# Random-feature attention, the queries' part: ScalarE copies a step's turned features ahead of the next exponentials, VectorE divides one step later

## Chip, cores and metric

The kernel runs on one core of a Trainium2 chip. The time is the device time of one execution in microseconds (us); a kernel's time is the median over its runs.

## What is computed

The reference runs a graph transformer over 1250 nodes of width 512: a layer norm, then a four-layer graph network and, beside it, a "performer" block, and last a mixture of experts. The change is in the performer's attention. Cut to it (8 heads of width 64, 256 random features):

```
def softmax_kernel(x, pmat):
    xp = jnp.einsum('bhnd,df->bhnf', x, pmat)
    xp = xp - jnp.max(xp, axis=-1, keepdims=True)
    return jnp.exp(xp) / math.sqrt(pmat.shape[-1])
...
q_prime = softmax_kernel(q, Pmat)
k_prime = softmax_kernel(k, Pmat)
kv = jnp.einsum('bhnf,bhne->bhfe', k_prime, v)
k_sum = jnp.sum(k_prime, axis=2) + 1e-06
z = 1.0 / jnp.einsum('bhnf,bhf->bhn', q_prime, k_sum)[..., None]
attn = jnp.einsum('bhnf,bhfe->bhne', q_prime, kv) * z
...
x = x + attn @ Wproj + bproj
```

## The kernel before

The program has three stages, one after another, with a barrier of all engines between them: performer(), gnn() and moe(). Within a stage each engine has its own list of instructions, written out by hand, and the lists are tied together by counting semaphores: `then_inc` at a producer, `wait_ge` at a consumer. No scheduler moves anything; an engine runs its list strictly in order, so what stands ahead of an instruction in its list holds it up.

In performer(), attention_pe(), attention_dve() and attention_act() hold the lists of TensorE, VectorE and ScalarE for the attention. First come 20 steps over the keys, which end in the 256 x 64 sums kv and k_sum of each head, turned and copied to SBUF. Then come the 20 steps over the queries (Q_STEPS), with which the change has to do. A step is two heads (one g) and two tiles of 125 nodes (one u). For step n:

- F(n), features(n), TensorE, helper line L956: the queries by the random matrix, into two PSUM banks, n % 2 choosing which two. It waits for E(n-2), which read those banks.
- M(n), highest(n), VectorE, L1096: the negated maximum of each row of 256.
- E(n), ScalarE, L1150: four exponentials with the maximum as bias, into the SBUF buffer kf, two deep. It waits for M(n) and for T(n-2).
- T(n), turn_features(n), TensorE, L1022: eight transposes of the features into PSUM banks 4 and 5. These two banks are not doubled, so that T(n) waits for C(n-1) as well as for E(n).
- C(n), ScalarE, L1144: two copies of the turned features to qf_cols in SBUF, two deep. It waits for T(n) and for A(n-2).
- A(n), attend(n), TensorE, L1037: the products with kv and with k_sum, into bank 6 or 7. It waits for C(n) and, by `out_made`, for D(n-2).
- D(n), divide(n), VectorE, L1108 and L1110: the reciprocal of the denominators and the multiplication into cols.

TensorE's list has, in round n, F(n), T(n-1), A(n-2). After the last round come the projection of the first node tile (project_pe(0), L1061), T(19), project_pe(1), A(18), A(19), and then pe_end() with further projections; VectorE adds each projection to the residual (project_dve, L1070). The letters F, M, E, T, C, A, D are used in all that follows.

Of the kernel before, what the change touches and what calls it, by code (L numbers as in the profile page):

```python
# [144 lines left out]
def performer(c, xbuf, gnn_x, xn_dram, sum_dram, ln_count, cond_parts, cond_w_parts, w, cols, rows,  # L145
# [62 lines left out]
    qf_mm, qf_max, qf_made, qf_turned, qf_cols_made = c.sems("p_qf_mm", "p_qf_max", "p_qf_made", "p_qf_turned",  # L208
                                                             "p_qf_cols_made")
    out_mm, den_made, out_made = c.sems("p_out_mm", "p_den_made", "p_out_made")  # L210
# [4 lines left out]
    with ExitStack() as ctx:  # L215
# [55 lines left out]
        qf_cols = shared[:, 0:2 * 4 * 2 * P].rearrange("p (u e a n) -> p u e a n", u=2, e=2, a=2)  # L271
# [39 lines left out]
        def split_dve(i):  # L311

            v = c.dve
            which, i = divmod(i, 5)
            rest, parts = ((cond[:, :], c_split), (cond_w, w_split))[which]
            if which == 0 and i == 0:
                v.wait_ge(cond_made, 3)
                v.wait_ge(q_mm, GROUPS)
            if which == 1 and i == 0:
                v.wait_ge(cond_w_in, 128)  # L320
            if i % 2 == 0:
                if i:
                    v.wait_ge(split_step, 2 * which + i // 2)
                v.tensor_copy(parts[i // 2], rest).then_inc(part_made, 1)
            else:
                v.wait_ge(part_made, 3 * which + i // 2 + 1)
                v.tensor_tensor(rest, rest, parts[i // 2], ALU.subtract).then_inc(split_step, 1)
# [613 lines left out]
        def kf_out(n):  # L941

            return psum[0:P, 2 * (n % 3) * BANK:(2 * (n % 3) + 2) * BANK].rearrange("p (e a f) -> p e a f", e=2, a=2)

        def qf_out(n):

            return psum[0:P, 2 * (n % 2) * BANK:(2 * (n % 2) + 2) * BANK].rearrange("p (e a f) -> p e a f", e=2, a=2)

        def qf_turned_out(e):
            return psum[0:128, (4 + e) * BANK:(4 + e) * BANK + 4 * P].rearrange("p (a n) -> p a n", a=2)  # L950

        def kf_slot(n, e, b):
            return 4 * (n % 2) + 2 * e + b
# [111 lines left out]
        def project_dve(t):  # L1065
            v = c.dve
            if t == 0:
                v.wait_ge(bp_added, NT)
            v.wait_ge(o_mm, t + 1)
            v.tensor_tensor(x[:, t, :], x[:, t, :], c.bank(t % 2, D, P), ALU.add).then_inc(o_added, 1)  # L1070
            v.wait_ge(o_added, t + 1)
            h_stats_dve(t)

        def attention_dve():
            v = c.dve
            for n in range(K_STEPS + S_LAG):
                if n < K_STEPS:
                    v.wait_ge(kf_mm, n + 1)
                    if n >= 2:
                        v.wait_ge(kf_made, 4 * (n - 1))  # L1080
                    v.tensor_reduce(mx[:, 4 * (n % 2):4 * (n % 2) + 4].rearrange("p (e a) -> p e a", e=2), kf_out(n), AX.X,
                                    ALU.max, negate=True).then_inc(kf_max, 1)
                if n % 2 == 1 and n // 2 < 10:
                    split_dve(n // 2)
                g, u = divmod(n - K_LAG + 1, NT // 2)
                if u == 0 and 1 <= g <= G:
                    v.wait_ge(kv_mm, g * (NT // 2))
                    v.tensor_copy(kv_t[:, g - 1, 0:F], c.bank(6, F)).then_inc(kv_made, 1)
                g, u = divmod(n - S_LAG + 1, NT // 2)
                if u == 0 and 1 <= g <= G:  # L1090
                    v.wait_ge(ks_mm, g * (NT // 2))
                    v.tensor_scalar(kv_t[:, g - 1, F:2 * F], c.bank(7, F), K_SUM_SMALL, None, ALU.add).then_inc(ks_made, 1)

            def highest(n):
                v.wait_ge(qf_mm, n + 1)
                v.tensor_reduce(mx[:, 4 * (n % 2):4 * (n % 2) + 4].rearrange("p (e a) -> p e a", e=2), qf_out(n), AX.X,  # L1096
                                ALU.max, negate=True).then_inc(qf_max, 1)

            def divide(n):

                g, u = divmod(n, NT // 2)
                at = (6 + n % 2) * BANK
                v.wait_ge(out_mm, n + 1)
                if n == 0:
                    v.wait_ge(parts_in, 192)
                else:
                    v.wait_ge(out_made, n)
                v.reciprocal(rden, psum[0:128, at + 2 * P:at + 4 * P]).then_inc(den_made, 1)  # L1108
                v.wait_ge(den_made, n + 1)
                v.tensor_tensor(cols[:, g, 2 * u * P:2 * (u + 1) * P], psum[0:128, at:at + 2 * P], rden,  # L1110
                                ALU.mult).then_inc(out_made, 1)

            for n in range(Q_STEPS):
                highest(n)
                if n >= 2:
                    divide(n - 2)
            project_dve(0)
            divide(Q_STEPS - 2)
            project_dve(1)
            divide(Q_STEPS - 1)  # L1120

        def attention_act():
            s = c.act
            s.wait_ge(c.slots_blank, 16)
            for n in range(K_STEPS):
                s.wait_ge(kf_max, n + 1)
                if n >= 2:
                    s.wait_ge(kv_mm, n - 1)
                    s.wait_ge(kf_summed, n - 1)
                for b in range(2):  # L1130
                    for e in range(2):
                        at = 4 * (n % 2) + 2 * e + b
                        s.activation(kf[:, kf_slot(n, e, b), :], kf_out(n)[:, e, b, :], ACT.Exp,
                                     bias=mx[:, at:at + 1]).then_inc(kf_made, 1)
            for g in range(G):
                s.wait_ge(kv_turned, g + 1)
                s.copy(kv_flat[:, g, :], c.bank(g)).then_inc(kv_cols_made, 1)
            for n in range(Q_STEPS + 2):
                if n >= 2:
                    if n >= 4:  # L1140
                        s.wait_ge(out_mm, n - 3)
                    for e in range(2):
                        s.wait_ge(qf_turned, 2 * n - 3 + e)
                        s.copy(qf_cols[:, n % 2, e], qf_turned_out(e)).then_inc(qf_cols_made, 1)  # L1144
                if n < Q_STEPS:
                    s.wait_ge(qf_max, n + 1)
                    if n >= 2:
                        s.wait_ge(qf_turned, 2 * (n - 1))
                    for i in range(4):
                        s.activation(kf[:, 4 * (n % 2) + i, :], qf_out(n)[:, i // 2, i % 2, :], ACT.Exp,  # L1150
                                     bias=mx[:, 4 * (n % 2) + i:4 * (n % 2) + i + 1]).then_inc(qf_made, 1)
# [305 lines left out]

        attention_pe()
        attention_dve()
        attention_act()  # L1460
        attention_pool()
        sp_end()
# [1282 lines left out]
```

## Time and profile before

| | |
|---|---|
| median of 3 runs | 2674.96 us (2674.15 to 2680.72) |
| the profiled execution's own time | 2671.21 us |
| its span, first to last instruction | 2669.5 us |
| mean granted clock of TensorE | 0.988 of full speed |
| TensorE matmuls busy | 2578.7 us, 97% |
| VectorE busy | 1396.1 us, 52% |
| ScalarE busy | 850.7 us, 32% |
| GpSimd busy | 397.7 us, 15% |

The busy times are sums over the whole span. The queries' steps take the stretch from about 248 us to 350 us of it, some 4% of the kernel; whether TensorE is busy in that stretch is read from the stretch itself and not from the mean.

### The profile page before, as it was taken

The page shows a single profiled execution, that of the slowest core. Times are in us where ns is not written, and L with a number is a line of the kernel's source. Part 1 is how long each engine was busy: PE and PEld are TensorE (multiplying, and loading weights), DVE is VectorE, ACT ScalarE, POOL GpSimd, SP SyncE. Part 2 cuts the span into 40 slices and gives each one's busy share as a digit, 9 for nine tenths or more (in the row PEclk, how much of TensorE's full clock was granted, in tenths as well). Part 3 has the DMA queues.
Part 4 walks back from the last instruction along what each step waited for, and adds up shares of the span by engine and source line. Part 5 has one row for each costly group of instructions (what it writes and reads, how often), then busy time and mean ns, then how long its engine had stood idle before and what let it go on. Part 6 is the DMA issues. An engine that isn't in the chain of part 4 may idle for free. (4 is left out here: it accounts for less than half of the span.)

```text
span 2669.5 us, 29597 instructions
## 1 busy us (share of the span) xinstructions
PE 2578.7 (97%) x10736; PEld 1534.9 (57%) x10736; DVE 1396.1 (52%) x3067; ACT 850.7 (32%) x1775; POOL 397.7 (15%) x396
## 2 busy tenths in 40 slices
PE   8999899999999999999999999999999998999994
PEld 4665545456776555777555677655577754533341
DVE  7986741515665532666551566653266654523344
ACT  5875532212442120444111244312044412302221
POOL 2004120102000200200200200020020012515551
PEclk9999999999999999999999999999999999999997
DMA  6301011420000110000010000011000001569636
GB/s 172 121 21 48 1 43 45 114 67 24 1 1 1 41 36 23 18 1 1 22 39 32 24 1 1 1 41 36 18 22 1 1 17 55 189 198 328 215 89 212
DMA packets 84372, 154.71 MB, mean 58 GB/s; under 512 B 31909, under 2 KB 32389, under 8 KB 81887
## 3 DMA queue, kind: packets, MB, share of 16 engines
q1 hardware_dynamic: 60702, 106.12, 12.8%
q0 software_dynamic: 20784, 41.80, 4.8%
q10 hardware_dynamic: 2741, 4.89, 0.7%
q8 instruction: 87, 1.43, 0.2%
q14 instruction: 58, 0.48, 0.1%
HBM read 207.61 MB, written 27.34 MB: 88 GB/s over the span
## 5 line engine op out<-in xcount | busy, mean ns | idle before, releaser
L1942 ACT ACTIVATE g_prob<-g_prob,g_row_max 125x1250 f32<-125x1250 f32 x160 | 214.0, 1338 | 710.6 <-DVE g_row_max L1876 710.6
L1682 PE MATMUL psum<-cols,w 128*128 128x500 f32 (+1 forms) x1120 | 393.2, 510 | 1.2 <-PEq L88 1.2
L1744 PE MATMUL psum<-g_k_cols,g_q_cols 128*125 128x512 f32 (+1 forms) x960 | 362.9, 513 | 1.9 <-DVE g_row_max L1873 1.9
L1758 PE MATMUL psum<-cols,rows 125*128 125x250 f32 x1600 | 364.0, 374 | 0.1
L1758 PEld LDWEIGHTS psum<-cols,rows 125*128 125x128 f32 x1600 | 302.7, 189 | 34.6 <-issue 3.8
L1682 PEld LDWEIGHTS psum<-cols,w 128*128 128x128 f32 x1120 | 209.9, 189 | 173.1 <-issue 165.0
L1873 DVE CUSTOM_DVE_ANT_0 g_prob<-psum,ln_count 125x1250 f32<-125x1250 f32 x160 | 233.5, 1459 | 75.2 <-PE psum L1744 75.2
L1744 PEld LDWEIGHTS psum<-g_k_cols,g_q_cols 128*125 128x125 f32 x960 | 168.0, 187 | 161.8 <-issue 159.1
L1883 DVE COPY cols<-psum 125x500 f32<-125x500 f32 x160 | 108.6, 679 | 199.2 <-PE psum L1773 199.2
L1773 PEld LDWEIGHTS psum<-ident,g_prob 125*125 125x125 f32 x1600 | 199.4, 188 | 9.0 <-issue 1.9
L1996 POOL TENSOR_TENSOR xbuf<-xbuf,g_bias_rows 125x512 f32<-125x512 f32 x40 | 63.2, 1618 | 937.0 <-DVE rows L1617 937.0
L1773 PE MATMUL psum<-ident,g_prob 125*125 125x125 f32 x1600 | 200.3, 272 | 0.0
L2527 PE MATMUL psum<-m_ew,m_x_cols 128*64 128x256 f32 (+1 forms) x576 | 155.5, 503 | 3.1 <-DMA cols<-in_L_ffn_expert_w,m_weights_of 2.8
L1848 DVE TENSOR_SCALAR g_k_cols<-psum,g_bias_cols 128x500 f32<-128x500 f32 (+1 forms) x48 | 31.3, 652 | 228.7 <-PE psum L1682 228.7
L1866 DVE TENSOR_SCALAR g_prob<-g_prob,g_row_max 125x1250 f32<-125x1250 f32 x160 | 144.8, 905 | 5.6
L1992 POOL TENSOR_TENSOR xbuf<-xbuf,g_bias_rows 125x512 f32<-125x512 f32 x40 | 54.9, 1412 | 606.1 <-DMA g_bias_rows<-in_L_gnn_bo 606.1
L1784 PE MATMUL psum<-w,g_q_cols 128*125 128x512 f32 x320 | 143.9, 592 | 0.0
L1830 PE MATMUL psum<-w,g_k_cols 128*125 128x512 f32 x320 | 143.6, 592 | 0.0
L1958 ACT COPY cols<-psum 125x500 f32<-125x500 f32 x320 | 134.2, 469 | 17.6 <-PE psum L1773 16.9
L1731 PE MATMUL psum<-w,cols 128*125 128x512 f32 x320 | 139.3, 592 | 0.0
L2573 DVE TENSOR_TENSOR m_work<-psum,m_eb 128x768 f32<-128x768 f32 x27 | 41.0, 1518 | 151.0 <-PE psum L2527 141.9
L1731 PEld LDWEIGHTS psum<-w,cols 128*125 128x125 f32 x320 | 60.0, 187 | 71.8 <-issue 71.5
(346 smaller groups left out, 3446.7 us busy)
## 6 DMA issues: line engine op xcount, KB each, us to landing
m_eb<-in_L_ffn_expert_b SPq DMA_DIRECT2D x54, 192.0 KB, 5.8
w<-in_L_gnn_m_w SPq DMA_DIRECT2D x8, 1024.0 KB
slot_rows<-p_kf SPq DMA_DIRECT2D x1, 7128.0 KB, 33.5
rows<-slot_rows SPq DMA_DIRECT2D x54, 132.0 KB, 3.4
m_ew<-in_L_ffn_expert_w SPq DMA_DIRECT2D x4, 1536.0 KB, 11.0
w<-in_L_mix_W SPq DMA_DIRECT2D x4, 1024.0 KB, 5.1
w<-in_L_gnn_wq SPq DMA_DIRECT2D x4, 1024.0 KB, 5.3
w<-in_L_gnn_wk SPq DMA_DIRECT2D x4, 1024.0 KB
```

The costliest lines, as they stand in the source:

```text
L1682: ins = c.pe.matmul(c.bank(group_bank(g), width), wt[:, k, o * 128:(o + 1) * 128], y_cols[:, k, start:start + width], start=(k == 0), stop ...
L1731: ins = pe.matmul(c.bank(V_BANKS[t], D, P), y_cols[:, k, t * P:(t + 1) * P], w[2][:, k, :], start=(k == 0), stop=(k == KC - 1))
L1744: ins = pe.matmul(psum[0:P, start:start + width], q_cols[:, h, t * P:(t + 1) * P], k_cols[:, h, start:start + width], start=True, stop=True)
L1758: ins = pe.matmul(c.bank(6 + g % 2, 2 * P), v_rows[:, j, h * 128:(h + 1) * 128], turned_prob[:, g % 2, j, :], start=(j == 0), stop=(j == N ...
L1773: ins = pe.transpose(psum[0:P, b * BANK + j * P:b * BANK + (j + 1) * P], prob[:, u, (j0 + j) * P:(j0 + j + 1) * P], ident[0:P, 0:P])
L1784: ins = pe.matmul(c.bank(t % 2, D, P), q_cols[:, k, t * P:(t + 1) * P], w[0][:, k, :], start=(k == 0), stop=(k == KC - 1))
L1830: ins = pe.matmul(c.bank(t % 2, D, P), k_cols[:, k, t * P:(t + 1) * P], w[2][:, k, :], start=(k == 0), stop=(k == KC - 1))
L1866: v.tensor_scalar(prob[:, u, :], prob[:, u, :], row_max[:, u, 3:4], None, ALU.mult).then_inc(prob_made, 1)
L1873: v.tensor_tensor_reduce(prob[:, u, :], psum[0:P, 0:N], ln_count[:, t, :], 1.0, NOT_AN_EDGE / 10, ALU.add, ALU.max, row_max[:, u, 0:1]).th ...
L1942: s.activation(prob[:, u, :], prob[:, u, :], ACT.Exp, bias=row_max[:, u, 1:2], accum_out=row_max[:, u, 2:3]).then_inc(exp_made, 1)
L1958: s.copy(turned_prob[:, g % 2, j0:j0 + nj, half:half + P], by_chunk(c.bank(b, nj * P, P))).then_inc(turned_act, 1)
L2527: ins = pe.matmul(psum[lanes(e), at:at + cn], x_cols[u][:, k, lanes(e)], ew1[s][:, k, c0:c0 + cn], start=(k == 0), stop=(k == KC - 1))
```

## The change

ScalarE's loop now has C(n-1) ahead of E(n), where it had C(n-2). VectorE's loop has D(n-3) behind M(n), where it had D(n-2), and the left-over D(17) stands ahead of the projection's addition. TensorE's list, the buffers, the PSUM banks and each instruction's operands are as they were. The counts that C waits for follow the renumbering: for a given step they are the same as before.

```
             for n in range(Q_STEPS):
                 highest(n)
-                if n >= 2:
-                    divide(n - 2)
+                if n >= 3:
+                    divide(n - 3)
+            divide(Q_STEPS - 3)
             project_dve(0)
             divide(Q_STEPS - 2)
             project_dve(1)
...
-            for n in range(Q_STEPS + 2):
-                if n >= 2:
-                    if n >= 4:
-                        s.wait_ge(out_mm, n - 3)
+            for n in range(Q_STEPS + 1):
+                if n >= 1:
+                    if n >= 3:
+                        s.wait_ge(out_mm, n - 2)
                     for e in range(2):
-                        s.wait_ge(qf_turned, 2 * n - 3 + e)
-                        s.copy(qf_cols[:, n % 2, e], qf_turned_out(e)).then_inc(qf_cols_made, 1)
+                        s.wait_ge(qf_turned, 2 * n - 1 + e)
+                        s.copy(qf_cols[:, (n - 1) % 2, e], qf_turned_out(e)).then_inc(qf_cols_made, 1)
                 if n < Q_STEPS:
                     s.wait_ge(qf_max, n + 1)
                     if n >= 2:
```

How the instructions stand on ScalarE at the beginning of the queries' steps, before the change (p_kf is the features' buffer, p_shared holds qf_cols, p_mx the maxima):

```order
L1150 ACTIVATE p_kf<-psum,p_mx 125x256 [waits p_qf_max]
L1150 ACTIVATE p_kf<-psum,p_mx 125x256 x3
L1150 ACTIVATE p_kf<-psum,p_mx 125x256 [waits p_qf_max]
L1150 ACTIVATE p_kf<-psum,p_mx 125x256 x3
L1144 COPY p_shared<-psum 128x500 [waits p_qf_turned] x2
L1150 ACTIVATE p_kf<-psum,p_mx 125x256 [waits p_qf_turned,p_qf_max]
L1150 ACTIVATE p_kf<-psum,p_mx 125x256 x3
```

The same place after the change:

```order
L1151 ACTIVATE p_kf<-psum,p_mx 125x256 [waits p_qf_max]
L1151 ACTIVATE p_kf<-psum,p_mx 125x256 x3
L1145 COPY p_shared<-psum 128x500 [waits p_qf_turned] x2
L1151 ACTIVATE p_kf<-psum,p_mx 125x256 [waits p_qf_max]
L1151 ACTIVATE p_kf<-psum,p_mx 125x256 x3
L1145 COPY p_shared<-psum 128x500 [waits p_qf_turned] x2
L1151 ACTIVATE p_kf<-psum,p_mx 125x256 [waits p_qf_turned,p_qf_max]
```

The two copies of step 0 moved from behind the exponentials of step 1 to ahead of them, and so with every later step: ScalarE's list is now E(0), C(0), E(1), C(1), E(2).

On VectorE the same place, before the change (rows holds the reciprocals, cols the result):

```order
L1096 TENSOR_REDUCE p_mx<-psum 125x4 [waits p_qf_mm] x3
L1108 RECIPROCAL rows<-psum 128x250 [waits parts_in,p_out_mm]
L1110 TENSOR_TENSOR cols<-psum,rows 128x250 [waits p_den_made]
L1096 TENSOR_REDUCE p_mx<-psum 125x4 [waits p_qf_mm]
L1108 RECIPROCAL rows<-psum 128x250 [waits p_out_made,p_out_mm]
L1110 TENSOR_TENSOR cols<-psum,rows 128x250 [waits p_den_made]
```

And after it:

```order
L1096 TENSOR_REDUCE p_mx<-psum 125x4 [waits p_qf_mm] x4
L1108 RECIPROCAL rows<-psum 128x250 [waits parts_in,p_out_mm]
L1110 TENSOR_TENSOR cols<-psum,rows 128x250 [waits p_den_made]
L1096 TENSOR_REDUCE p_mx<-psum 125x4 [waits p_qf_mm]
L1108 RECIPROCAL rows<-psum 128x250 [waits p_out_made,p_out_mm]
L1110 TENSOR_TENSOR cols<-psum,rows 128x250 [waits p_den_made]
```

One more maximum stands ahead of the first division, so that each division is of a step one further back.

## Rows read from the trace of the kernel before

**Rows 1.** Busy time by stretches: length, each engine, TensorE's granted clock, DMA

```profile
252.90:256.40 3.50, 3.50 (x16) 2.49 (x16) 1.23 (x1) 1.60 (x4) 0.00 (x0) 0.51 0.33 128
318.00:326.93 8.93, 7.86 (x65) 5.14 (x65) 6.55 (x7) 5.02 (x12) 0.00 (x0) 1.00 0.00 0
331.00:2260.00 1929.00, 1921.74 (x7324) 1200.21 (x7323) 973.60 (x1902) 546.67 (x1091) 158.15 (x114) 1.00 0.08 25
```

**Rows 2.** Waits of TensorE from 251 to 331 us: total us, times, longest

```profile
PE psum L1022 <- ACT p_shared L1144: 8.6, 8, 1.1
```

**Rows 3.** Waits of the other engines from 251 to 335 us

```profile
ACT p_kf L1150 <- DVE p_mx L1096: 36.4, 18, 3.2
...
DVE rows L1108 <- PE psum L1037: 21.6, 18, 2.4
```

**Rows 4.** Timeline of two steps: start, length, engine [idle before <-releaser]

```profile
291.22 1.04 PE L1022 MATMUL psum<-ident,p_kf 125*128 125x125 f32 x8 [1.07 <-ACT p_shared L1144]
291.23 1.22 DVE L1096 TENSOR_REDUCE p_mx<-psum 125x4 f32<-125x1024 f32 x1
...
292.19 1.91 PE L1037 MATMUL psum<-p_shared 128*64 128x250 f32 x16
292.48 1.57 ACT L1150 ACTIVATE p_kf<-psum,p_mx 125x256 f32<-125x256 f32 x4 [1.40 <-DVE p_mx L1096]
293.92 1.07 ACT L1144 COPY p_shared<-psum 128x500 f32<-128x500 f32 x2
...
294.04 1.13 PE L956 MATMUL psum<-p_pmat,p_q_cols 64*125 64x256 f32 x8
294.15 1.72 DVE L1108 RECIPROCAL rows<-psum 128x250 f32<-128x250 f32 x1 [1.71 <-PE psum L1037]
...
295.13 1.04 PE L1022 MATMUL psum<-ident,p_kf 125*128 125x125 f32 x8
...
296.25 1.22 DVE L1096 TENSOR_REDUCE p_mx<-psum 125x4 f32<-125x1024 f32 x1
297.50 1.56 ACT L1150 ACTIVATE p_kf<-psum,p_mx 125x256 f32<-125x256 f32 x4 [2.51 <-DVE p_mx L1096]
...
298.93 1.07 ACT L1144 COPY p_shared<-psum 128x500 f32<-128x500 f32 x2
...
300.15 1.04 PE L1022 MATMUL psum<-ident,p_kf 125*128 125x125 f32 x8 [1.07 <-ACT p_shared L1144]
```

**Rows 5.** Timeline of the first steps

```profile
250.18 3.02 ACT L1150 ACTIVATE p_kf<-psum,p_mx 125x256 f32<-125x256 f32 x8 [1.59 <-DVE p_mx L1096]
...
251.80 1.07 PE L1022 MATMUL psum<-ident,p_kf 125*128 125x125 f32 x8 [2.02 <-ACT p_kf L1150]
...
252.80 1.94 PE L956 MATMUL psum<-p_pmat,p_q_cols 64*125 64x256 f32 x8
253.04 1.10 ACT L1144 COPY p_shared<-psum 128x500 f32<-128x500 f32 x2
...
254.68 1.89 PE L1022 MATMUL psum<-ident,p_kf 125*128 125x125 f32 x8
254.78 1.23 DVE L1096 TENSOR_REDUCE p_mx<-psum 125x4 f32<-125x1024 f32 x1 [3.51 <-PE psum L956]
...
259.39 1.07 PE L1022 MATMUL psum<-ident,p_kf 125*128 125x125 f32 x8
```

**Rows 6.** Timeline of the last steps and what follows

```profile
330.83 1.05 PE L1022 MATMUL psum<-ident,p_kf 125*128 125x125 f32 x8
...
337.18 1.02 PE L1022 MATMUL psum<-ident,p_kf 125*128 125x125 f32 x8
...
337.87 1.05 ACT L1144 COPY p_shared<-psum 128x500 f32<-128x500 f32 x2 [2.16 <-PE psum L1022]
...
350.32 0.62 PE L759 MATMUL psum<-ident,p_kf 125*128 125x125 f32 x4 [1.52 <-DVE p_kf L731]
```

**Rows 7.** Waits of TensorE from 345 to 2263 us, the longest group of four

```profile
PE psum L1577 <- DVE rows L1607: 2.7, 2, 2.5
```

## The prediction, made before the changed kernel ran

> **What bounds the kernel now.** I read the stretches first, then the waits of TensorE, then the timeline of two steps, then both ends of the queries' part. From 331 to 2260 us TensorE's matmuls are busy for 1921.74 of 1929.00 us at a granted clock of 1.00 [rows 1]: behind the attention the program is TensorE from end to end, so that it can only be moved as a whole. In two steps of the queries, 318.00 to 326.93 us, TensorE is busy for 7.86 of 8.93 us, VectorE for 6.55 and ScalarE for 5.02 [rows 1]. No engine is full there, so the steps hang on hand-overs. TensorE's waits say on which: eight times, 8.6 us together, a T waits for a copy by ScalarE [rows 2]. ScalarE in its turn waits 36.4 us for the maxima, and VectorE's reciprocals wait 21.6 us for attend [rows 3].
>
> The timeline shows the ring [rows 4]. Counting back from the last in-loop T, which is T(18) at 330.83 us [rows 6], the T at 291.22 is T(9), the one at 295.13 T(10), the one at 300.15 T(11). T(10) follows T(9) after 3.91 us with no wait; T(11) follows T(10) after 5.02 us, of which 1.07 is the wait for C(10) at 298.93. C(10) stands behind E(11), E(11) at 297.50 has waited 2.51 us for M(11), and M(11) started at 296.25 although its features, the F at 294.04 of 1.13 us, were there at 295.17: VectorE was in D(8), whose reciprocal had itself waited 1.71 us for A(8), the matmuls at 292.19. So the division sits ahead of a maximum that is ready, and E sits ahead of a copy that is ready. The period is 300.15 - 291.22 = 8.93 us for two steps, 4.465 a step.
>
> **What the change does, part by part.** It adds and removes no instruction on any engine and issues no DMA; SyncE's and GpSimd's queues are untouched. It moves two C copies per step and one D per step.
>
> *TensorE's own pace.* Where it does not wait, its round is T to A 0.97 (291.22 to 292.19), A to F 1.85 (292.19 to 294.04), F to T 1.09 (294.04 to 295.13): 3.91 us [rows 4]. This is the new period if the two other engines are quicker.
>
> *ScalarE's ring after the change* is T(n-1), C(n-1), E(n), T(n), all in series, a chain that did not exist before. T's start to C's start, where C waited for it, is 337.87 - 337.18 = 0.69 us, since the first copy needs only half of the transposes; the copies take 1.05 [rows 6]. From the start of E(0) at 250.18 to T(0) at 251.80, where T waited for it, is 1.62 us [rows 5]. Sum 3.36 us, 0.55 below 3.91. With C now ahead of E, what stands behind the waiting copy on ScalarE is E(n), and T(n) waits for that; the cover for it is A(n-2) and F(n+1) on TensorE, 1.85 + 1.09 = 2.94 us. If the ring were longer than 3.91, every 0.1 us over would cost 16 x 0.1 = 1.6 us.
>
> *VectorE's ring.* From the reciprocal at 294.15 to the next maximum at 296.25 is 2.10 us, the maximum takes 1.22: 3.32 us a step [rows 4], 0.59 below 3.91. D(n-3) now follows M(n), and A(n-3) stood ahead of F(n) on TensorE, so the reciprocal no longer waits. M(n) can start 0.04 us behind F(n) (254.78 against 252.80 + 1.94 = 254.74 [rows 5]) and ends 1.26 us behind it. E(n) waits for C(n-1), which ends 0.69 + 1.05 = 1.74 us behind T(n-1)'s start, that is behind F(n)'s end to within 0.04: so the maximum is 0.4 to 0.5 us early and drops out of the ring.
>
> *What the later division could delay.* A(n-2) waits for D(n-4). D(n-4) ends 1.26 + 2.10 = 3.4 us behind F(n-1)'s end, A(n-2) starts one round and a T behind it, 3.91 + 0.97 = 4.9 us. 1.5 us to spare, cost nothing; without that cover each step would pay what is missing.
>
> *The start.* T(0) stays at 251.80 us: nothing ahead of it moves. C(0) can start at 252.49 and end at 253.54; only then E(1), which before ran straight behind E(0). T(1) comes 1.62 - 0.07 us later (I let E overlap the copy's end a little), at about 255.1, where it was at 254.68: 0.4 us late. TensorE's clock was at 0.51 of full between 252.90 and 256.40 us [rows 1], behind an idle time of 2.02 us before T(0) [rows 5]; at such a clock T(1) took 1.89 instead of 1.04. Started 0.4 later it has less of the slow stretch to go through, if that ends when it did, so T(2) is late by 0.25 us; if the slow stretch ends later too, by 0.45. I take 0.3.
>
> *The steady steps.* T(2) was at 259.39 [rows 5], T(18) at 330.83 [rows 6]: 71.44 us for 16 steps. At 3.91 they take 62.56. Gain 8.88 us, which is the eight waits of 1.07 [rows 2] and a little of restarting.
>
> *The end.* Behind T(18) TensorE has A(17), the projection, T(19), the projection, A(18), A(19): it did not wait there for the moved work, since the first idle time is the 1.52 us before 350.32, for VectorE's norm behind D(19) [rows 6]. D(17) has its place ahead of the first projection's addition in both lists. M(19) is only earlier. Everything keeps its distance from T(18), and I count nothing.
>
> *Behind it.* What TensorE waits for up to 2263 us is little, the longest group being 2.7 us, and none of the four groups is a DMA [rows 7]; the loads are issued by SyncE behind events of this same program and move along. The gain reaches the end whole.
>
> Sum: -8.88 + 0.3 = -8.6 us. The profiled execution had 2671.21 us (span 2669.5), so it would have 2662.6. The median of the runs shown is 2674.96, 3.75 above the profiled one; I carry the difference over: **2666.4 us**, 0.32% less. The least change that a measurement here tells from none is about 0.3%, which is 8.0 us: the forecast lies right at this edge.
>
> **A rule to weigh.** TensorE's matmuls look busy without a break through a round of 3.91 us, while its weight loads fill 5.14 of 8.93 us [rows 1]. The Trainium skill, "Perfetto Trace Analysis", section Identifying the Most-Contended Engine, says that matmul busy time is no good measure of how near TensorE is to its limit, since pipelined matmuls look otherwise in a trace than they are, and that weight-load time is the better one. By the row the round costs 3.91 us and the sum is -8.6; by that rule TensorE would have room left, which is the second rival below. The trace speaks for the row: every second round ran without any wait and none came in under 3.9 us.
>
> **The rivals.**
> (a) *ScalarE's new ring is longer than TensorE's round.* The parts were read where other engines were idle; if the hand-overs together cost 0.85 us more, the ring is 4.2 us, the gain 16 x (4.465 - 4.2) - 0.3 = 3.9 us: 2671 us. For it: the ring is in series now. Against it: four hand-overs and a slack of 0.55 that already includes the measured ones. Chance 0.09.
> (b) *TensorE is not the limit at 3.91.* Then the step falls to ScalarE's 3.36: 16 x (4.465 - 3.36) - 0.3 = 17.4 us gained, 2657.6 us. Against it the unwaited rounds. Chance 0.03.
> (c) *The change does not do what it says*, because the period is held by something that I read as released, and stays at 4.46: 2675 us. Chance 0.04.
> (d) *Slower, by the clock.* T(1) now has to wait for E(1) with TensorE idle for some 0.3 us within the slow stretch. If TensorE then stays at its lower level, 1.2 GHz, a step costs up to twice 3.91 (T took 1.89 and F 1.94 us there [rows 5]): 3.7 to 3.9 us more each. Three such steps eat the gain; five give about +10 us, 2685 us, and slower by over 0.3% begins at (8.6 + 8.0) / 3.8 = 4.4 steps. Against it: in the steps from T(3) on the clock was 1.00 in spite of a gap of 1.07 us in every second one [rows 1, 4], and such gaps are what the change takes away. Chance 0.04.
>
> **How the numbers follow.** The forecast has 0.80. Its own range comes from the start (0.25 to 0.45 us), the round (3.90 to 3.93, 0.3 us over 16) and the scatter of medians, about 1.5 us (the three runs lie between 2674.15 and 2680.72): 2664.5 to 2668.5. About five eighths of it lie beyond the 8.0 us. Faster by over 0.3%: 0.50 + 0.03 (b) = 0.53. Within 0.3%: 0.30 + 0.09 + 0.04 = 0.43. Slower: 0.04. The range to be given takes in half of (a) and leaves out (b), (c) and (d): 2663 to 2672.
>
> **What the profile after would show.** Right: consecutive T's 3.9 us apart from T(2) to T(18), T(18) near 322.3 us, no wait of a T for a copy, the reciprocals' waits for attend gone, ScalarE's wait for the maxima nearly gone and in its place a wait of C for T; ScalarE idle about 0.55 us before the copies. T(1) near 255.1. The norm's wait of 1.5 us behind D(19) unchanged. Wrong: a T that waits for E (then ScalarE's ring is the period), a granted clock below 1.00 between 260 and 322 us, an A that waits for a division, or a new wait of TensorE behind 350 us.

## The result, and the profile after

The changed kernel has a median of 2667.11 us over 10 runs (2657.04 to 2669.89), the kernel before 2674.82 us over 10 runs: 7.7 us less by the medians, and a ratio of 0.9966, 95% interval 0.9957 to 0.9976, which is 9.1 us (6.4 to 11.5). Faster, by 0.34%; whether by more than the 0.3% that the prediction named is left open by the interval (0.24% to 0.43%). The profiled execution has a span of 2664.7 us, 4.8 us less than that of before (2669.5): about half of what the queries' steps gained in it, and the section below on the last stage says why.

Busy time by stretches of the changed kernel (length, TensorE, its weight loads, VectorE, ScalarE, GpSimd, granted clock, DMA share, GB/s). The second row is two rounds and answers to the second of [rows 1]:

```profile
252.90:256.40 3.50, 2.98 (x16) 2.01 (x12) 1.22 (x1) 2.31 (x6) 0.00 (x0) 0.52 0.33 129
314.03:321.85 7.82, 7.82 (x67) 5.14 (x65) 6.54 (x6) 5.04 (x12) 0.00 (x0) 1.00 0.00 0
...
322.00:2251.00 1929.00, 1921.50 (x7322) 1199.70 (x7322) 974.12 (x1902) 546.69 (x1091) 157.66 (x114) 1.00 0.08 25
```

Two rounds take 7.82 us instead of 8.93, and TensorE is busy for all of them. The work is the same (7.86 us of TensorE then, 7.82 now); only the 1.07 us of waiting is gone. The third row is the same 1929 us of program as the third of [rows 1]: TensorE does 1921.50 us of work in it, then 1921.74.

The waits of TensorE from 251 to 322 us, whole, answer to [rows 2]:

```profile
PE psum L1022 <- ACT p_kf L1151: 2.5, 2, 2.0
```

No T waits for a copy any more. The two waits that are left are those of T(0) and T(1) for exponentials. Waits of the other engines from 251 to 335 us, against [rows 3]:

```profile
ACT p_shared L1145 <- PE psum L1022: 29.4, 20, 3.8
...
DVE p_mx L1096 <- PE psum L956: 17.0, 18, 4.0
...
DVE rows L1108 <- PE psum L1037: 4.3, 1, 4.3
```

ScalarE no longer waits for maxima (36.4 us before) but for the transposes, VectorE no longer waits for A but for F. (The one wait for A that is left, 4.3 us, is that of D(18), behind the steps; the kernel before has it too, 4.25 us at 343.53.) Both now wait for the engine that sets the pace. One round in the timeline (start, length, engine, line, in brackets the idle time before), against [rows 4]:

```profile
290.59 1.07 PE L1022 MATMUL psum<-ident,p_kf 125*128 125x125 f32 x8
290.71 1.23 DVE L1096 TENSOR_REDUCE p_mx<-psum 125x4 f32<-125x1024 f32 x1 [0.60 <-PE psum L956]
291.33 1.05 ACT L1145 COPY p_shared<-psum 128x500 f32<-128x500 f32 x2 [1.39 <-PE psum L1022]
...
291.60 1.91 PE L1037 MATMUL psum<-p_shared 128*64 128x250 f32 x16
291.85 1.71 DVE L1108 RECIPROCAL rows<-psum 128x250 f32<-128x250 f32 x1
292.27 1.58 ACT L1151 ACTIVATE p_kf<-psum,p_mx 125x256 f32<-125x256 f32 x4
...
293.44 1.13 PE L956 MATMUL psum<-p_pmat,p_q_cols 64*125 64x256 f32 x8
...
294.50 1.07 PE L1022 MATMUL psum<-ident,p_kf 125*128 125x125 f32 x8
```

T to T is 3.91 us. The copies start 0.74 us behind T, the exponentials 0.94 us behind the copies, and they are done at 293.85, where the next T has its turn only at 294.50: the 0.6 us that ScalarE has to spare. The beginning, against [rows 5]:

```profile
251.44 1.07 PE L1022 MATMUL psum<-ident,p_kf 125*128 125x125 f32 x8 [2.02 <-ACT p_kf L1151]
252.12 1.05 ACT L1145 COPY p_shared<-psum 128x500 f32<-128x500 f32 x2 [0.73 <-PE psum L1022]
...
252.44 1.73 PE L956 MATMUL psum<-p_pmat,p_q_cols 64*125 64x256 f32 x8
253.06 1.58 ACT L1151 ACTIVATE p_kf<-psum,p_mx 125x256 f32<-125x256 f32 x4
...
254.70 1.81 PE L1022 MATMUL psum<-ident,p_kf 125*128 125x125 f32 x8 [0.52 <-ACT p_kf L1151]
...
259.34 1.07 PE L1022 MATMUL psum<-ident,p_kf 125*128 125x125 f32 x8
```

T(1) now waits for E(1), which stands behind C(0): T(0) to T(1) is 3.26 us, before 2.88. The end, against [rows 6]:

```profile
321.85 1.07 PE L1022 MATMUL psum<-ident,p_kf 125*128 125x125 f32 x8
...
328.23 1.02 PE L1022 MATMUL psum<-ident,p_kf 125*128 125x125 f32 x8
...
341.37 0.62 PE L759 MATMUL psum<-ident,p_kf 125*128 125x125 f32 x4 [1.53 <-DVE p_kf L731]
```

T(2) to T(18) is 62.51 us (71.44 before), T(18) to the first transposes of the norm 19.52 us (19.49 before), and these wait for the norm as they did. Everything ahead of the queries' steps was 0.36 us earlier in this execution (T(0) at 251.44, 251.80 before), which is none of the change's doing; from T(0) to T(18) it is 79.03 us before and 70.41 us now: 8.62 us. Behind 330 us the longest wait of TensorE up to 2250 us, against [rows 7]:

```profile
PE psum L1745 <- DVE g_row_max L1874: 1.9, 4, 0.5
```

No new wait came up there.

### The profile page after: what moved, and what is told of

It reads as the page before. It is cut to its first block and busy times, and to the rows that moved or that the text cites. A ratio compares the mean times of both kernels' runs of the same rounds, so it can differ in the third digit from the quotient of the medians.

```text
span 2664.7 us, 29597 instructions
## 1 busy us (share of the span) xinstructions
PE 2578.3 (97%) x10736; PEld 1534.4 (58%) x10736; DVE 1397.4 (52%) x3067; ACT 851.2 (32%) x1775; POOL 397.3 (15%) x396
## 3 DMA queue, kind: packets, MB, share of 16 engines
q8 instruction: 87, 1.43, 0.2%
```

## The experiments

Two questions. The first: do the two moves each take away a wait of their own, or is there one ring through both, which either opens? And what holds the steps at 3.91 us now? The second: where are the 4 us that the profiled execution lost behind the attention? One more kernel starts the queries' part earlier.

The table has what the traces of all kernels show: from the start of the transposes of the key sums (line L1001 of the kernel before) to T(0), T(0) to T(1), T(2) to T(18), and the last part of the last stage, from the first L2527 (its number moves with the edits) to the end of the span. Each is the difference of two starts in the timeline.

| kernel | key sums to T(0) | T(0) to T(1) | T(2) to T(18) | last part |
|---|---|---|---|---|
| before | 5.96 | 2.88 | 71.44 | 296.6 |
| before_look1 | 5.96 | 2.49 | 71.44 | 301.5 |
| before_look2 | 5.95 | 3.68 | 71.41 | 305.6 |
| changed | 5.95 | 3.26 | 62.51 | 301.5 |
| after_again | 5.95 | 3.26 | 62.50 | 302.9 |
| scalar_only | 5.96 | 3.26 | 63.39 | 300.1 |
| vector_only | 5.95 | 2.88 | 63.29 | 301.3 |
| after_half | 5.96 | 3.26 | 53.06 | 288.4 |
| scalar_half | 5.96 | 3.25 | 56.66 | 288.9 |
| vector_half | 5.96 | 2.49 | 56.54 | 288.4 |
| after_ballast1 | 5.96 | 4.19 | 62.67 | 302.7 |
| after_ballast2 | 5.96 | 4.21 | 68.62 | 306.0 |
| early_start | 1.91 | 3.43 | 63.32 | 303.7 |
| early_full | 1.91 | 3.43 | 62.51 | 301.3 |

### The changed kernel again

> The changed kernel once more, so that its time and trace stand beside the other kernels of this series on one chip. Both theories: T(2) to T(18) takes 62.5 us, the time is 7 to 9 us under the kernel before. If the 4 us that the first profile showed less than the steps had gained belong to the change, the last stage (from the first L2528 to the end) takes about 301 us again; if they are scatter of the last stage, it lies somewhere between 296 and 302 us.

Median 2668.5 us over 9 runs against 2675.35 of before in the same series; ratio 0.9974, interval 0.9964 to 0.9984. The steps take 62.50 us, as foretold. The gain of this series is 7.0 us by the ratio, of the first 9.1; the intervals overlap, and the 8.6 us of the steps lie in both (6.4 to 11.5, and 4.3 to 9.6). The last part takes 302.9 us.

### Each half alone

ScalarE's order alone is the changed kernel with VectorE's loop put back:

```
             for n in range(Q_STEPS):
                 highest(n)
-                if n >= 3:
-                    divide(n - 3)
-            divide(Q_STEPS - 3)
+                if n >= 2:
+                    divide(n - 2)
             project_dve(0)
```

> Only ScalarE's order is changed, VectorE divides where it did before. Theory 1 (one ring): in the kernel before, two rounds are one ring, D(8) 2.10, M(11) 1.26, E(11) 1.44, C(10) 1.07, T(11) 0.97, A(10) 1.85 us and hand-overs, 8.93 together, and it takes either move to open it. Without the copy behind the exponentials the ring D, M, E, T, A is 2.10 + 1.26 + 1.62 + 0.97 + 1.85 = 7.8 us for two rounds, just under TensorE's 2 x 3.91 = 7.82: T(2) to T(18) takes 62.5 to 63 us, T(1) is late by 0.3 to 0.4 us, and the time is that of the full change within 1 us, 8 us under before. Theory 2 (each move removes its own wait): about half of the gain, T(2) to T(18) 66 to 68 us, 4 us under before.

VectorE's order alone is the kernel before with the same lines turned the other way round, and ScalarE's loop untouched.

> Only VectorE's order is changed, ScalarE copies where it did before. Theory 1 (one ring): with the division out of it, F(11), M(11), E(11), C(10), T(11) with A is 1.13 + 1.26 + 1.44 + 1.07 + 0.97 + 1.85 = 7.7 us for two rounds, under 7.82: T(2) to T(18) takes 62.5 to 63 us, T(1) stays where it was before the change (2.9 us behind T(0), not 3.26), and the time is that of the full change or up to 0.4 us under it, 8.5 to 9 us under before. Theory 2 (each move removes its own wait): about half of the gain, T(2) to T(18) 66 to 68 us, 4 us under before.

scalar_only: 2669.77 us over 12 runs, ratio 0.9978 (0.9968 to 0.9989). vector_only: 2668.24 us over 8 runs, ratio 0.9968 (0.9956 to 0.998). The whole change in the same series: 0.9974. By times the three can't be told apart; by the traces either half brings T(2) to T(18) from 71.44 to 63.3 or 63.4, that is 8.1 us of the 8.9. Theory 2, half and half, is out. The timeline of scalar_only shows what is left:

```profile
285.15 1.07 PE L1022 MATMUL psum<-ident,p_kf 125*128 125x125 f32 x8
...
286.15 1.91 PE L1037 MATMUL psum<-p_shared 128*64 128x250 f32 x16
286.30 1.22 DVE L1096 TENSOR_REDUCE p_mx<-psum 125x4 f32<-125x1024 f32 x1
287.55 1.57 ACT L1150 ACTIVATE p_kf<-psum,p_mx 125x256 f32<-125x256 f32 x4 [0.60 <-DVE p_mx L1096]
...
287.99 1.13 PE L956 MATMUL psum<-p_pmat,p_q_cols 64*125 64x256 f32 x8
288.11 1.72 DVE L1108 RECIPROCAL rows<-psum 128x250 f32<-128x250 f32 x1 [0.60 <-PE psum L1037]
...
289.17 1.07 PE L1022 MATMUL psum<-ident,p_kf 125*128 125x125 f32 x8
...
290.20 1.21 DVE L1096 TENSOR_REDUCE p_mx<-psum 125x4 f32<-125x1024 f32 x1
291.45 1.57 ACT L1150 ACTIVATE p_kf<-psum,p_mx 125x256 f32<-125x256 f32 x4 [0.49 <-DVE p_mx L1096]
...
293.07 1.07 PE L1022 MATMUL psum<-ident,p_kf 125*128 125x125 f32 x8
```

VectorE still waits for A and ScalarE for the maximum, in every round, and T to T is 4.02 and 3.90 us in turn. The ring leads from T at 285.15 through A at 286.15, the reciprocal at 288.11, the maximum at 290.20 and the exponentials at 291.45 to T at 293.07: 7.92 us for two rounds, a hair over twice 3.91, so that it holds the pace by some 0.05 us a step. And vector_only, through the copy:

```profile
285.38 1.05 PE L1022 MATMUL psum<-ident,p_kf 125*128 125x125 f32 x8
285.47 1.23 DVE L1096 TENSOR_REDUCE p_mx<-psum 125x4 f32<-125x1024 f32 x1 [0.69 <-PE psum L956]
...
286.73 1.57 ACT L1151 ACTIVATE p_kf<-psum,p_mx 125x256 f32<-125x256 f32 x4 [1.49 <-DVE p_mx L1096]
288.17 1.07 ACT L1145 COPY p_shared<-psum 128x500 f32<-128x500 f32 x2
...
289.38 1.04 PE L1022 MATMUL psum<-ident,p_kf 125*128 125x125 f32 x8
```

The copy ends at 289.24 and T follows at 289.38: here the ring T, A, F, M, E, C takes 7.91 us for two rounds. I had expected 7.8 and 7.7 for the two rings and so no more than 63 us; the hand-overs between the engines, most of which I had left out of the sums, made the 0.1 to 0.2 us of the difference.

The ring of the kernel before reads from [rows 4]: reciprocal to maximum 2.10, maximum to exponentials 1.25, exponentials to copies 1.43, copies to T 1.22, T to A 0.97, A to reciprocal 1.96, together 8.93 us for two rounds. That this is the period is no proof: the pieces are start-to-start times that follow on one another, so that they close by construction. What speaks for the ring is that each link is either a wait that the link before ended, or an instruction directly behind it on its engine, and that both rounds always add up: in before_look2 they take 4.92 and 4.01 us in turn, in the first profile 5.02 and 3.91, together 8.93 in both. It is tested by the kernels that open it, above, and by those that shorten one link of it, below.

### Half of A left out

```
-                for sums in range(2):
+                for sums in range(1):
...
-                v.reciprocal(rden, psum[0:128, at + 2 * P:at + 4 * P]).then_inc(den_made, 1)
+                v.reciprocal(rden, psum[0:128, at:at + 2 * P]).then_inc(den_made, 1)
```

> The changed kernel with half of each A left out: the products with k_sum are not made, and the reciprocal is taken of the numerators instead of the denominators, so that the attention's result is not the reference's. TensorE's round loses 8 of A's 16 matmuls, 0.92 us: 2.99 instead of 3.91. If TensorE's round is what holds the steps at 3.91 us, the period falls until the next ring holds it: ScalarE's T, C, E by the trace of the changed kernel, 0.74 + 0.94 + 1.62 = 3.30 us, or VectorE's 3.91 - 0.60 = 3.31; T(2) to T(18) takes 53 to 54 us instead of 62.5, and T now waits for E. If something else holds 3.91 (a hand-over that I read as free), it stays near 62.5.

> ScalarE's order alone, with half of each A left out as in after_half (no products with k_sum, the reciprocal of the numerators, so the attention's result is not the reference's). In the trace of scalar_only the ring through the division reads R to M 2.09, M to E 1.25, E to T 1.62, T to A 1.00, A to R 1.96, 7.92 us for two rounds. With 0.92 less of A it is 7.0: 3.50 us a step, T(2) to T(18) 56.0 us, against 53.1 of after_half: the second move is then worth 2.9 us, where it was worth 0.9. If the two moves are worth the same whatever TensorE's round is, 54 us.

> VectorE's order alone, with half of each A left out in the same way. The ring through the copy reads in the trace of vector_only T to A 0.98, A to F 1.84, F to M 1.18, M to E 1.26, E to C 1.44, C to T 1.21, 7.91 us for two rounds; with 0.92 less of A 6.99: 3.50 us a step, T(2) to T(18) 56.0 us. If the two moves are worth the same whatever TensorE's round is, 54 us.

after_half takes 53.06 us for the 16 steps, 3.32 each, instead of 62.5. TensorE's round held the 3.91: with a shorter round the steps follow, until ScalarE's ring stops them. Its timeline:

```profile
283.13 1.07 PE L1022 MATMUL psum<-ident,p_kf 125*128 125x125 f32 x8 [0.19 <-ACT p_kf L1151]
283.87 1.05 ACT L1145 COPY p_shared<-psum 128x500 f32<-128x500 f32 x2 [0.79 <-PE psum L1022]
...
284.81 1.58 ACT L1151 ACTIVATE p_kf<-psum,p_mx 125x256 f32<-125x256 f32 x4
...
286.45 1.07 PE L1022 MATMUL psum<-ident,p_kf 125*128 125x125 f32 x8 [0.18 <-ACT p_kf L1151]
```

T to C 0.74, C to E 0.94, E to T 1.64: 3.32 us, and T waits 0.18 us for the exponentials each time. The forecast had this ring at 3.36. scalar_half and vector_half take 56.66 and 56.54 us, 3.54 and 3.53 a step. The 56.0 foretold was too low because the eight matmuls left out shorten the way from A to F not by 0.92 us but by 0.85 (from 1.84 to 0.99 in vector_half); 7.92 and 7.91 less 0.85 are, to within 0.01 us, the measured 7.08 and 7.07 us for two rounds. Under a shorter round the second move is worth 3.6 us (VectorE's) and 3.5 us (ScalarE's), under the real one 0.9 and 0.8. The two moves cover for each other only as long as TensorE's round is the longer one. The times of these three kernels (2642.03, 2649.69 and 2646.73 us, one run each) are lower by more than the steps are, and most of that lies in their last part, which takes 288 to 289 us. The attention's values are others in these kernels, and with them the experts' work may be; that this is the cause is not shown.

### More work in ScalarE's ring

```
                     for e in range(2):
                         s.wait_ge(qf_turned, 2 * n - 1 + e)
+                        for i in range(1 if e == 0 else 0):
+                            s.copy(edge_sum[:, 4 * P * i:4 * P * (i + 1)].rearrange("p (a n) -> p a n", a=2), qf_turned_out(e)[0:P])
                         s.copy(qf_cols[:, (n - 1) % 2, e], qf_turned_out(e)).then_inc(qf_cols_made, 1)
```

and the same with two copies.

> The changed kernel with one more copy of a turned half on ScalarE ahead of each C, into a buffer that nobody reads. By the rings: ScalarE's ring grows from 3.30 by one copy, 0.53 us, to 3.83, still under 3.91: T(2) to T(18) stays at 62.5 us. If ScalarE's new order has no such slack, each step grows by 0.5 us: 70 to 71 us.

> The same with two more copies for each C. By the rings: 3.30 + 2 x 0.53 = 4.36 us, over 3.91 by 0.45: T(2) to T(18) takes 69.5 to 70 us, T waits for E, and no wait for a copy shows. If the slack is larger than read, 62.5 us; if there was none, 78 to 79 us.

One copy more is free: 62.67 us. Two copies: 68.62 us, 4.29 a step, and T waits for E in every round, for the copies never (TensorE's waits from 262 to 327 us, some 15 rounds):

```profile
PE psum L1022 <- ACT p_kf L1153: 4.7, 15, 0.6
```

In its timeline the copies start at 287.46, the copies proper at 288.40, the exponentials at 289.34, and T runs from 286.72 to 291.00: 0.74 + 0.94 + 0.94 + 1.66 = 4.28. I had taken a copy at 0.53 us; in a row they follow each other after 0.47, hence 68.6 instead of 69.5 to 70. The slack of the new ring is real and lies between one copy and two, 0.47 and 0.94 us; 3.91 - 3.32 = 0.59 us fits. One run each: 2670.14 and 2679.86 us.

### An earlier start

TensorE is idle for 2.0 us ahead of T(0), and in the first profile its clock is low soon after. This kernel, on top of vector_only, takes F(0) and F(1) into the last rounds of the keys' loop, turns the key sums into banks 4 to 7, so that banks 0 to 3 are free for the features, and lets ScalarE make E(0) ahead of the copies of the key sums and E(1) between them:

```
+                if n in (K_STEPS, K_STEPS + 1):
+                    features(n - K_STEPS)
...
-                    ins = pe.transpose(c.bank(g)[:, n * 128:(n + 1) * 128], kv_t[:, g, n * 128:(n + 1) * 128], ident[:])
+                    ins = pe.transpose(c.bank(4 + g)[:, n * 128:(n + 1) * 128], kv_t[:, g, n * 128:(n + 1) * 128], ident[:])
...
+            exps(0)
             for g in range(G):
                 s.wait_ge(kv_turned, g + 1)
-                s.copy(kv_flat[:, g, :], c.bank(g)).then_inc(kv_cols_made, 1)
+                s.copy(kv_flat[:, g, :], c.bank(4 + g)).then_inc(kv_cols_made, 1)
+                if g == 1:
+                    exps(1)
```

> On top of the VectorE-only kernel: the features F(0) and F(1) and the maximum M(0) are made while the keys' last sums still run, the turned key sums go into banks 4 to 7 instead of 0 to 3, and E(0) and E(1) stand around the first two copies of these sums. The idle 2.0 us of TensorE before T(0) should go, and T(0) start some 3 us earlier against the transposes of the key sums (before: 6.0 us behind their start). If the low clock from 252.9 to 256.4 us follows from that idle time, F(2) and T(1) run at full speed, 1.13 and 1.04 us, which gives 1.6 us more: 4 to 5 us under the VectorE-only kernel. If the low clock comes from something else, 2 to 3 us under it. If the start is hidden anyway, no gain.

2665.09 us over 5 runs, ratio 0.9959 (0.9946 to 0.9971). That is 3.2 us under vector_only by the medians and 2.4 by the ratios, where 4 to 5 were foretold. From the key sums to T(18) it takes 72.54 us, vector_only 76.84, before 84.99, and T(0) comes 4.0 us earlier against the key sums. But this ruler flatters the edit: F(0) and F(1) now stand ahead of the transposes of the key sums, so that these start later. An instruction that the edit leaves where it was is the start of the keys' last exponentials, in vector_only and in early_start:

```profile
244.00 1.57 ACT L1134 ACTIVATE p_kf<-psum,p_mx 125x256 f32<-125x256 f32 x4 [0.43 <-DVE p_mx L1081]
```

```profile
244.37 1.57 ACT L1142 ACTIVATE p_kf<-psum,p_mx 125x256 f32<-125x256 f32 x4 [0.43 <-DVE p_mx L1091]
```

From there T(0) comes 7.42 us later instead of 10.03, and T(18) 78.05 instead of 80.92: the early start is worth 2.9 us in these two traces, not 4.3. No low clock shows in early_start; vector_only's profile had one (T(0) to T(2) 7.60 us), so a part of the 2.9 us is the clock's. And T(1) now waits 1.3 us for C(0), which stands behind two copies of key sums. With the full change's orders on top:

> The early start of the queries' part together with the full change (both orders) instead of VectorE's alone. The early start gave 4.3 us from the transposes of the key sums to T(18) (76.84 to 72.54 us), ScalarE's order gives T(2) to T(18) 62.5 instead of 63.3. Together 71.7 to 72 us from the transposes of the key sums to T(18), where the changed kernel has 76.4 and the kernel before 85.0: 4 to 5 us under the changed kernel, 12 to 13 us under before. If the last stage gives some of it back, as its waits for weights seemed to, 9 to 11 us under before.

2661.89 us over 6 runs, against 2675.11 in the same series: ratio 0.9949 (0.9935 to 0.9964), 13.6 us less (9.6 to 17.4). The key sums to T(18) take 71.72 us, as foretold by the same ruler; from the keys' last exponentials to T(18) it is 77.23 us, the changed kernel 80.44, before 89.07: 3.2 and 11.8 us. The 11.8 us lie within the interval. It is the fastest kernel of this study that computes the reference's result. Its start in the timeline:

```profile
248.87 1.97 PE L1013 MATMUL psum<-ident,p_shared 128*128 128x128 f32 x16
...
250.58 1.57 ACT L1153 ACTIVATE p_kf<-psum,p_mx 125x256 f32<-125x256 f32 x4
...
250.78 1.04 PE L1025 MATMUL psum<-ident,p_kf 125*128 125x125 f32 x8
...
251.76 1.13 PE L956 MATMUL psum<-p_pmat,p_q_cols 64*125 64x256 f32 x8
...
254.21 1.04 PE L1025 MATMUL psum<-ident,p_kf 125*128 125x125 f32 x8 [1.31 <-ACT p_shared L1168]
```

F(2) takes 1.13 and T(1) 1.04 us, full speed, where they took 1.94 and 1.89 [rows 5] (before_look1 has them at full speed too, without the early start).

### The kernel before, profiled twice more

> The kernel before once more, for a second look at its last stage: from the first L2527 to the end its first profile shows 296.6 us, with 9.2 us of waits for weights, and the kernels with a shorter queries' part show 300.1 to 303.7 us with 11.9 to 14.9 us. If an earlier arrival costs waits for weights there, this one shows about 296.6 us again. If it is scatter, it shows anything up to 303 us. T(2) to T(18) takes 71.4 us in both cases.

> The same, a third look at the kernel before: about 296.6 us from the first L2527 to the end if the earlier arrival is what costs, anything up to 303 us if it is scatter.

The last part takes 301.5 and 305.6 us, against 296.6 in the first profile, while the queries' steps take 71.44 and 71.41. So it was scatter: the first profile of before had a short last part, that of the changed kernel (301.5) is nothing special. Of TensorE's waits there, those for the experts' weights add up to 9.2 us in the first profile, 10.0 and 13.3 us in the two further ones, and 13.8 us in the changed kernel's. The rows of before_look2, waits of TensorE behind 2360 us:

```profile
PE psum L2527 <- DMA m_ew<-in_L_ffn_expert_w,m_weights_of: 7.0, 3, 2.9
PE psum L2527 <- DMA cols<-in_L_ffn_expert_w,m_weights_of: 6.3, 1, 6.3
```

These waits explain only a part of the scatter: the 9 us between the three profiles go with 4 us of them, and what makes the rest is open.

## Why the prediction was right, point by point

- *One ring through division, maximum, exponentials, copy and transposes.* Right, shown: either move opens it (63.3 and 63.4 us), and 0.85 us less of A shortens what each move alone leaves of it by 0.84 us for two rounds.
- *TensorE's own round of 3.91 us as the new period.* Right: 62.51 us for 16 steps, forecast 62.56. That TensorE's round is what holds it was shown by shortening A: 53.06 us. Rival (b), with room left in TensorE, is out; the rule of the Trainium skill that would have suggested it, "Perfetto Trace Analysis", section Identifying the Most-Contended Engine, does not hold as a limit here: weight loads fill only 5.14 of 7.82 us while TensorE has no wait at all. (The section names the share of peak FLOPs beside the weight loads; that was not worked out here.)
- *ScalarE's new ring 3.36 us, VectorE's 3.32.* Right: 3.32 and 3.31 (3.91 less VectorE's wait of 0.60). In the first, two small errors cancel: T to C is 0.74 us, not 0.69, and C to E 0.94, not 1.05. Rival (a), a ring longer than the round, did not come; the loaded ring showed that it needed more than one extra copy.
- *The later division delays no A.* Right: TensorE has no wait for a division.
- *The start costs 0.3 us.* Right: 8.93 - 8.62 = 0.31 us. T(1) comes 0.38 us late against T(0) (forecast 0.4). But the number holds only because the clock fell in both profiles. Before, T(0) to T(2) takes 7.59 us with the low clock and 6.36 without it (before_look1). With the change T(1) comes 3.26 us behind T(0) at either clock (after_half, at 1.00 throughout, has 3.26 too), and one round of 3.91 later T(2): 7.17 us at full clock. By this estimate the start costs 0.8 us in an execution without the low clock, and the gain is 8.1 us. That the two profiles compared were alike in this is luck.
- *The end and what lies behind it.* Right up to the last stage: T(18) to the norm is 19.52 against 19.49 us. At the first L2527 the changed kernel is 9.65 us ahead (2363.21 against 2372.86), of which 8.6 are the steps' and the rest is scatter ahead of and between the stages. What I did not have in the sum is the scatter of the last part, 9 us over three executions of one kernel. I carried a difference of 3.75 us between profile and median over as a constant; it probably belongs to that part, since 296.6 us is the shortest last part of the eleven profiles with the whole A. The profiled execution of the changed kernel took 2666.41 us, not the 2662.6 foretold for it.
- *The time.* For the median 2666.4 foretold, 2667.11 measured; a gain of 8.6 foretold, 9.1 and 7.0 by the two ratios. Whether it is over or under 0.3% was left nearly even, and two series still put it on both sides.
- *The clock staying low*, rival (d): did not happen; the clock is 1.00 from 256.4 us on.
- *What was not seen beforehand:* that the two moves are nearly redundant. The prediction took them as one and never summed the ring for each alone, though the rows for it were there. After the fact, 8.1 of the 8.9 us come with either.

## What to carry to other kernels

When several engines wait for each other and none is full, write down the ring: start to start, along the instruction that ended each wait, until it closes, with the number of rounds that it spans. That it sums to the period proves nothing, since it closes by construction; each link must be a wait ended by the link before, or an instruction directly behind it, and a kernel that takes a known time out of one link should shorten the period by just that. The new period is then the longest of the remaining rings and of each engine's own round, and moves that open the same ring do not add. Where two orders open the same ring, the one that puts nothing in series at the start (here the division's) is the cheaper one by the traces (T(0) to T(1) 2.88 against 3.26 us), and the second adds little (0.8 to 0.9 us of steps) until the bounding engine becomes faster. When a gain of a few us is to be read from one profile, read it at the end of the stage concerned, counted from an instruction that the edit does not move: here the last stage alone moves by 9 us from one execution of the same kernel to the next.

## What the runs showed of the hardware

TensorE's low clock at the start of the queries' part comes and goes. The same program, the same 2.02 us of idle time ahead of T(0): in the first profile of before the clock is 0.51 of full, the 1.2 GHz of the lower level, from 252.9 to 256.4 us, beginning 1.1 us behind T(0); in before_look1 it is 1.00 throughout; in before_look2 it is low from T(0) (250.45 us) on, as the rows below show (stretch, length, busy times, clock, DMA):

```profile
249.00:251.00 2.00, 0.55 (x3) 0.55 (x4) 0.93 (x1) 2.00 (x7) 0.00 (x0) 0.87 0.33 128
251.00:252.00 1.00, 1.00 (x7) 0.99 (x5) 0.00 (x0) 1.00 (x4) 0.00 (x0) 0.50 0.34 131
252.00:254.00 2.00, 2.00 (x10) 1.17 (x8) 0.00 (x0) 0.90 (x2) 0.00 (x0) 0.53 0.33 128
254.00:256.00 2.00, 2.00 (x18) 1.47 (x18) 1.22 (x1) 0.49 (x2) 0.00 (x0) 1.00 0.33 128
```

T(0) to T(2) takes 7.59 us in the first profile, 6.36 in before_look1, 7.71 in before_look2: the low stretch costs 1.2 to 1.35 us when it comes. Over all kernels here, 12 profiles have the idle 2.02 us ahead of T(0); seven of them show the low stretch, beginning with T(0) or some 1.2 us behind it, five do not (before_look1, after_half, scalar_half, vector_half, after_ballast2). The two profiles with the early start, where TensorE had no such idle time, show none, which against five of twelve says little: whether the idle time brings it on is open. The idle 1.07 us in every second round of the kernel before did not: its clock was 1.00 from 260 to 331 us.
